# A fused decoder layer on one core: the sixteen rounds of the cross attention in another order

## The chip, the core and the metric

The kernel runs on one core of a Trainium2 chip. The core has TensorE (PE in the profile; its weight loads are PEld), VectorE (DVE), ScalarE (ACT), GpSimd (POOL) and SyncE (SP, which only issues DMAs here). Each engine works through its own queue in order, and they meet in semaphores. The metric is the device time of one execution in microseconds, the median of several runs.

## The reference

A decoder layer on 32 blocks of 128 tokens, 512 channels, in float32:

```
x = x + self_attention(layernorm(x))            # differential attention, 32 score heads of 16
x = x + cross_attention(layernorm(x), ctx)      # 8 heads of 16, 512 positions, rotary
x = x + experts(layernorm(x))                   # 32 experts, 6 of 32 per token, and a shared expert
```

In the cross attention one block has queries, keys and values of 128 channels by 512 positions. Queries and keys are rotated (`t*cos + rot(t)*sin`), the scores are softmaxed over 512 keys, the values are weighted, and an output projection and the residual follow. The experts begin with a router: scores of 32 experts, the best 2 of 4 groups, the best 6 experts, their weights (a sigmoid, divided by the sum), and a place for each token in the list of each expert.

## The kernel before

The kernel has three parts: self attention (to about 750 us), cross attention (to about 1850 us), and the experts. The cross attention takes 32 blocks b, 16 rounds each: round n has b = n // 16 and r = n % 16. `cross_round` (line 151) lists the steps of round r, and every engine goes through this list and carries out its own piece of each step, in the order of the list. So the order in `cross_round` is the order of each engine's queue. A step that doesn't belong to an engine leaves its queue alone: two steps that change places in the list change nothing on an engine that has only one of them.

Every round has one `top` and one `score`. The rest is side work, which belongs to other blocks than the round's own (b + 1 is being prepared, b - 1 closed, b - 2 projected out, b - 3 and b - 4 routed). With T, S and so on as short names for what PE does:

- T, `top`: two matmuls of 512 columns (L765) into one of two pairs of banks; DVE takes the maxima of 1024 columns (L1409). T(n) waits until DVE has reduced T(n-2).
- S, `score`: two matmuls (L787) into banks 5 and 6; ACT takes the exponent of 1024 columns (PX, L1076). S(n) waits for the exponent of S(n-1): there is one pair of banks.
- A: weights times values (L804), behind every second S; `last` is the fourth A of a half block. ACT then copies bank 7 (`copy_v`, L1136).
- K, `keys_of`: six matmuls (L620 to L622 on CXS and WV); ACT writes vh (L1127).
- `rotate`: three matmuls, then a product on DVE (T1, L1434); GpSimd adds the two products (`total`, L1797); ACT rounds (`high`, L1119); GpSimd takes the rest (`low`, L1804). SP sends the parts to memory (`away`) and back in another layout (`stack`, 6 DMAs each for a quarter).
- `shares`, `sums`, `turn_g`: four transposes (L607). `expand` is ACT's copy rc (L1143) ahead of `shares`; DVE multiplies (on, L1445). `join` is the output projection, six matmuls. `maxima`: four transposes (L774), ACT copies (NT, L1070), SP writes a row.
- `norm_m`, `high_m`, `low_m`: the normalised x of a block (ACT, L1101), rounded (ACT, XMH, L1087), and the rest (GpSimd, xmL, L1814). `high_c`, `low_c` do the same for the context (ACT L1083, GpSimd CXS L1809), and `high_o`, `low_o` for the output (ACT OS L1095, GpSimd OS L1819).
- Router: `gate` (PE L862), `narrow` and `choose` (DVE, L1462 to L1485; the last three instructions of `choose` are L1479, L1483 and L1485), `weights` (DVE, from L1490), `rank`, `places`, and `spread` 0 to 5 (one indirect DMA of GpSimd each, L1829). `stats_g` and `stats_m`: bn_stats on DVE, three small instructions on GpSimd (ve, pow, sX or sY), `norm_g` or `norm_m` on ACT.

Bank 0 is shared by all side steps of PE: each waits until the reader of the step before it is done.

```
def bank0(signal, count):
    if zero["free"]:
        pe.wait_ge(*zero["free"])
    zero["free"] = (S[signal], count)
```

The two instructions of DVE and GpSimd that the prediction speaks of most are

```
dve.tensor_tensor(RM[:, 1 - d, :], RM[:, d, :], M[:, :], ALU.add)                      # L1485, end of choose
pool.tensor_tensor(xmL[:, :], xm[:, :], XMH[:, :].bitcast(f32), ALU.subtract)          # L1814, low_m
```

and GpSimd's `low_c` waits for ACT's `high_c` of the same block (`pool.wait_ge(S["a_ch"], b + 1)`).

Of the kernel before, what the change touches and what calls it, by code (L numbers as in the profile page):

```python
# [7 lines left out]
NB = 32  # L8
# [53 lines left out]
def self_part(do, do_cross):  # L62
# [3 lines left out]
    for w in range(-9, 2 * NB + 4):  # L66
# [26 lines left out]
        if e >= 4 * NB + 8 - AHEAD:  # L93
            for n in range(2):
                cross_round(do_cross, 2 * (e - (4 * NB + 8)) + n)
# [35 lines left out]
        if o >= 4 * NB + 8 - AHEAD:  # L131
            for n in range(2):
                cross_round(do_cross, 2 * (o - (4 * NB + 8)) + n)


def cross_part(do):


    for n in range(16 * NB + 14):
        cross_round(do, n)  # L140
# [10 lines left out]
def cross_round(do, n):  # L151
    b, r = divmod(n, 16)
    if r == 0:
        if 0 <= n - LAG < 16 * NB:
            do("score", n - LAG)
        do("stats_g", b + -3)
        do("stack", b + 0, 1, 1)
        do("keys_of", b + 0, 0)
        if 0 <= n < 16 * NB:
            do("top", n)  # L160
        do("expand", b + -2, 1)
    if r == 1:
        if 0 <= n < 16 * NB:
            do("top", n)
        if 0 <= n - LAG < 16 * NB:
            do("score", n - LAG)
        do("total", b + 1, 0)
        do("maxima", b + -1, 1)
        do("narrow", b + -4)
    if r == 2:  # L170
        if 0 <= n - LAG < 16 * NB:
            do("score", n - LAG)
        if 0 <= n < 16 * NB:
            do("top", n)
        do("rotate", b + 1, 0, 0)
        do("choose", b + -4)
    if r == 3:
        if 0 <= n - LAG < 16 * NB:
            do("score", n - LAG)
        do("rotate", b + 1, 0, 1)  # L180
        do("norm_g", b + -3)
        if 0 <= n < 16 * NB:
            do("top", n)
    if r == 4:
        if 0 <= n - LAG < 16 * NB:
            do("score", n - LAG)
        do("high", b + 1, 0)
        do("load_y", b + 2)
        do("last", b + -1, 0)
        do("shares", b + -2, 1)  # L190
        if 0 <= n < 16 * NB:
            do("top", n)
    if r == 5:
        if 0 <= n - LAG < 16 * NB:
            do("score", n - LAG)
        do("low", b + 1, 0)
        do("rotate", b + 1, 1, 0)
        do("copy_v", b + -1, 0)
        if 0 <= n < 16 * NB:
            do("top", n)  # L200
    if r == 6:
        if 0 <= n - LAG < 16 * NB:
            do("score", n - LAG)
        do("load_c", b + 2)
        do("rotate", b + 1, 1, 1)
        do("high_o", b + -2, 1)
        if 0 <= n < 16 * NB:
            do("top", n)
    if r == 7:
        if 0 <= n - LAG < 16 * NB:  # L210
            do("score", n - LAG)
        do("soften", b + -4)
        do("low_o", b + -2, 1)
        do("total", b + 1, 1)
        do("sums", b + -1, 0)
        do("weights", b + -4)
        if 0 <= n < 16 * NB:
            do("top", n)
    if r == 8:
        if 0 <= n - LAG < 16 * NB:  # L220
            do("score", n - LAG)
        do("low", b + 1, 1)
        do("rank", b + -4)
        if 0 <= n < 16 * NB:
            do("top", n)
        do("expand", b + -1, 0)
    if r == 9:
        if 0 <= n - LAG < 16 * NB:
            do("score", n - LAG)
        do("high", b + 1, 1)  # L230
        do("away", b + 1, 0)
        do("maxima", b + 0, 0)
        if 0 <= n < 16 * NB:
            do("top", n)
        do("stats_m", b + 2)
    if r == 10:
        if 0 <= n - LAG < 16 * NB:
            do("score", n - LAG)
        do("shares", b + -1, 0)
        do("places", b + -4)  # L240
        if 0 <= n < 16 * NB:
            do("top", n)
    if r == 11:
        if 0 <= n - LAG < 16 * NB:
            do("score", n - LAG)
        do("spread", b + -4, 0)
        do("low_o", b + -1, 0)
        do("high_o", b + -1, 0)
        do("turn_g", b + -3)
        do("spread", b + -4, 1)  # L250
        if 0 <= n < 16 * NB:
            do("top", n)
        do("spread", b + -4, 2)
    if r == 12:
        if 0 <= n - LAG < 16 * NB:
            do("score", n - LAG)
        do("away", b + 1, 1)
        do("stack", b + 1, 0, 0)
        do("stack", b + 1, 1, 0)
        do("norm_m", b + 2)  # L260
        do("gate", b + -3)
        if 0 <= n < 16 * NB:
            do("top", n)
    if r == 13:
        if 0 <= n - LAG < 16 * NB:
            do("score", n - LAG)
        do("keys_of", b + 0, 1)
        do("stack", b + 1, 0, 1)
        do("copy_v", b + -1, 1)
        do("last", b + -1, 1)  # L270
        do("spread", b + -4, 3)
        if 0 <= n < 16 * NB:
            do("top", n)
        do("spread", b + -4, 4)
    if r == 14:
        if 0 <= n - LAG < 16 * NB:
            do("score", n - LAG)
        if 0 <= n < 16 * NB:
            do("top", n)
        do("join", b + -2)  # L280
        do("low_c", b + 2)
        do("low_m", b + 2)
        do("high_c", b + 2)
    if r == 15:
        if 0 <= n < 16 * NB:
            do("top", n)
        if 0 <= n - LAG < 16 * NB:
            do("score", n - LAG)
        do("sums", b + -1, 1)
        do("high_m", b + 2)  # L290
        do("spread", b + -4, 5)
    piece, at = divmod(n - (16 * NB - 80), 8)
    if at == 0 and 0 <= piece < 8:
        do("land", piece // 4, piece % 4)
    if n == 16 * NB - 8:
        do("rows", 0)
    if 16 * NB <= n < 16 * NB + 12:
        do("split", 0, 1)
    if 16 * NB + 12 <= n < 16 * NB + 14:
        do("split", 1, 6)  # L300
# [1903 lines left out]
```

## Time and profile before

| | us |
|---|---|
| median of 3 runs | 3828.13 (3823.77 to 3829.65) |
| the profiled execution | 3817.57 |
| its span | 3815.8 |
| one block in the middle of the cross attention | 32.95 |
| in it busy: PE / DVE / ACT / GpSimd | 32.01 / 29.16 / 25.46 / 18.30 |

A timeline row gives the start from the span's start, the duration, engine, line, operation, and in brackets the idle time before it and what ended that. Rows that follow each other closely and are alike are merged (x2, x4, x8); one float32 matmul of A or `gate` stands as two. An instruction starts up to 0.1 us before the one in front of it has ended, so intervals are taken from start to start.

### The profile page before, as it was taken

To read this page: it belongs to the slowest core of one execution; us is meant where nothing else is said; L and a number is where in the kernel's file an instruction comes from. 1 tells how busy PE (TensorE), PEld (TensorE's weight loads), DVE (VectorE), ACT (ScalarE), POOL (GpSimd) and SP (SyncE) were. 2 spreads that over 40 slices of the span, in tenths; PEclk is the share of its full clock that TensorE was granted. 3 is DMA by queue.
4 is the path that set the end of the run, shared out by engine and by line. 5 is a ranking of instruction groups with operands and counts; after the bars stand their busy time and mean duration, and the time that the engine had idled before them with its cause. 6 is when DMAs were issued, how large, how long until landed. Compare 5 with 4: busy or idle time off the path is not lost.

```text
span 3815.8 us, 74126 instructions
## 1 busy us (share of the span) xinstructions
PE 3668.1 (96%) x24778; PEld 2905.2 (76%) x24778; DVE 2883.4 (76%) x5969; ACT 2352.5 (62%) x5418; POOL 1812.3 (47%) x2121
## 2 busy tenths in 40 slices
PE   6999999789999999999899999999999999999999
PEld 6888888534444444444589999999999999999998
DVE  5888888578888888888457777777777777777333
ACT  5888888457777777777435555555555555555121
POOL 2333332334555555554326666665666665555210
PEclk9999999789999999999899999999999999999999
DMA  5000000133334444443149999999999999998421
GB/s 209 24 25 28 27 26 21 42 108 123 127 124 133 133 128 127 131 154 121 48 141 265 263 268 263 266 268 266 264 267 264 268 265 265 267 262 239 154 84 58
DMA packets 290168, 621.37 MB, mean 163 GB/s; under 512 B 70000, under 2 KB 78576, under 8 KB 289664
## 3 DMA queue, kind: packets, MB, share of 16 engines
q1 hardware_dynamic: 224640, 464.01, 37.1%
q0 software_dynamic: 64000, 150.52, 16.4%
q8 instruction: 203, 3.33, 0.4%
q10 hardware_dynamic: 1152, 2.10, 0.2%
q14 instruction: 173, 1.42, 0.1%
HBM read 459.93 MB, written 155.98 MB: 161 GB/s over the span
## 4 chain that ended last, share of the span: by engine, by line
PE 82%; ACT 7%; DVE 6%; issue 3%; SPq 2%; DMA 1%; POOL 0%; DVEq 0%; ACTq 0%; POOLq 0%
PE ps L620 18%; PE ps L622 17%; PE ps L621 17%; PE ps L804 7%; PE ps L607 4%; PE ps L765 4%; ACT PA L1009 4%; PE ps L787 4%; PE ps L725 2%; PE ps L898 2%; PE ps L924 2%; PE ps L647 2%; ACT PX L1076 1%; DVE NM L1409 1%; DVE WD L1557 1%
## 5 line engine op out<-in xcount | busy, mean ns | idle before, releaser
L620 PE MATMUL ps<-WG,XT 128*128 128x352 f32 x2304 | 765.9, 332 | 7.3 <-DVE XT L1586 4.8
L621 PE MATMUL ps<-WG,XT 128*128 128x352 f32 x2304 | 744.7, 323 | 0.0
L622 PE MATMUL ps<-WG,XT 128*128 128x352 f32 x2304 | 744.6, 323 | 0.0
L1409 DVE TENSOR_REDUCE NM<-ps 128x2 f32<-128x1024 f32 x512 | 614.2, 1217 | 98.9 <-PE ps L765 92.4
L1076 ACT ACTIVATE PX<-ps 128x1024 f32<-128x1024 f32 x512 | 523.4, 1022 | 198.7 <-PE ps L787 184.2
L1903 POOL DMA_INDIRECT sum<-YO,TI x224 | 401.3, 1792 | 488.6 <-issue 393.8
L1222 ACT ACTIVATE HS<-ps 128x352 f32<-128x352 f32 x288 | 133.6, 464 | 561.7 <-PE ps L622 561.7
L1592 DVE TENSOR_TENSOR HS<-ps,HS 128x352 f32<-128x352 f32 x288 | 150.9, 524 | 426.1 <-ACT HS L1222 422.7
L1550 DVE TENSOR_TENSOR WG<-WL,WG 128x704 fp32r<-128x704 f32 x528 | 449.7, 882 | 28.3 <-ACT WG L1189 28.2
L620 PEld LDWEIGHTS ps<-WG,XT 128*128 128x128 f32 x2304 | 434.5, 189 | 9.3 <-DVE XT L1586 6.5
L621 PEld LDWEIGHTS ps<-WG,XT 128*128 128x128 f32 x2304 | 435.0, 189 | 0.0
L622 PEld LDWEIGHTS ps<-WG,XT 128*128 128x128 f32 x2304 | 434.3, 189 | 0.0
L1189 ACT ACTIVATE WG<-WL 128x704 fp32r<-128x704 f32 x528 | 395.2, 789 | 14.1 <-DMA DL<-in_w_down 13.9
L1009 ACT ACTIVATE PA<-ps,nb 128x128 f32<-128x128 f32 x1024 | 358.0, 381 | 1.2 <-DVE nb L1278 1.2
L620 PE MATMUL ps<-WD,HT 128*128 128x512 f32 (+1 forms) x864 | 344.9, 399 | 12.3 <-DVE HT L1598 12.3
L622 PE MATMUL ps<-WD,HT 128*128 128x512 f32 (+1 forms) x864 | 341.6, 395 | 0.0
L621 PE MATMUL ps<-WD,HT 128*128 128x512 f32 (+1 forms) x864 | 341.0, 395 | 0.0
L1885 POOL DMA_INDIRECT XI<-x_normed,TI x224 | 278.7, 1244 | 80.7 <-POOL TI L1880 61.8
L1213 ACT ACTIVATE XT<-ps 128x512 fp32r<-128x512 f32 x224 | 133.3, 595 | 245.2 <-PE ps L898 238.9
L804 PE MATMUL ps<-PX,vh 128*32 128x512 f32 x2048 | 278.8, 617 | 0.0
L1557 DVE TENSOR_TENSOR WD<-DL,WD 128x1024 fp32r<-128x1024 f32 (+1 forms) x264 | 240.0, 950 | 47.9 <-ACT WD L1196 47.8
L765 PE MATMUL ps<-KS,QS 48*128 48x512 f32 x1024 | 243.6, 484 | 14.3 <-DMA QS<-kq_parts 9.1
(275 smaller groups left out, 8530.8 us busy)
## 6 DMA issues: line engine op xcount, KB each, us to landing
WL<-in_w_gate SPq DMA_DIRECT2D x128, 704.0 KB, 4.2
WL<-in_w_up SPq DMA_DIRECT2D x128, 704.0 KB, 6.0
DL<-in_w_down SPq DMA_DIRECT2D x128, 512.0 KB, 8.4
kq_parts<-HL SPq DMA_DIRECT2D x64, 512.0 KB, 3.0
KS<-kq_parts SPq DMA_DIRECT2D x384, 64.0 KB, 2.3
QS<-kq_parts SPq DMA_DIRECT2D x384, 64.0 KB, 2.4
DL<-in_w_down SPq DMA_DIRECT2D x128, 192.0 KB, 9.2
CB<-sum POOLq DMA_DIRECT2D x64, 256.0 KB, 3.0
```

Of the source, the lines that this page charges most:

```text
L620: pe.matmul(out_, lh(0), rh(0), start=first, stop=False)
L621: pe.matmul(out_, lh(0), rh(1), start=False, stop=False)
L622: return pe.matmul(out_, lh(1), rh(0), start=False, stop=last)
L765: e = pe.matmul(bank(1 + 2 * (n % 2) + i), QS[64 * i:64 * i + 48, d, pp, 128 * qc:128 * qc + 128], KS[64 * i:64 * i + 48, d, pp, :], start ...
L804: e = pe.matmul(ps[32 * j:32 * j + 32, 7 * 512:8 * 512], vh[:, b % 2, sc, 4 * hh + j, :], PX[:, (8 * g + 2 * sc + j // 2) % 4, j % 2, :], ...
L1009: e = act.activation(PA[:, d, h, :], sums[:, h, :], ACT.Exp, bias=nb4[:, d, h:h + 1], scale=0.25, accum_out=SU[:, 8 * u + h:8 * u + h + 1])
L1076: act.activation(PX[:, n % 4, :, :], ps[:, 5 * 512:7 * 512], ACT.Exp, scale=0.25).then_inc(S["a_px"], 1)
L1189: act.activation(WG[q][:, 0, w, c:c + 2, :], WL[:, q, w, c:c + 2, :], ACT.Copy).then_inc(S["a_sp"], 1)
L1409: dve.tensor_reduce(NM[:, g % 2, qc, p:4:2], ps[:, 512 * bk:512 * bk + 1024].rearrange("p (i k) -> p i k", k=512), AX.X, ALU.max, negate=T ...
L1550: dve.tensor_tensor(WG[q][:, 1, w, c:c + 2, :], WL[:, q, w, c:c + 2, :], WG[q][:, 0, w, c:c + 2, :].bitcast(f32), ALU.subtract).then_inc(S ...
L1885: pool.indirect_dma_start(out=XI[:, t % NX, :], out_offset=None, in_=XN[:, :], in_offset=bass.IndirectOffsetOnAxis(ap=TI[:, r % 8:r % 8 + ...
L1903: pool.indirect_dma_start(out=AC[r % 2][:, :], out_offset=bass.IndirectOffsetOnAxis(ap=TI[:, r % 8:r % 8 + 1], axis=0), in_=YO[:, o % NO, ...
```

## The change

Only `cross_round` changes; no instruction is added or taken out. `keys_of` of half 0 moves from round 0 to round 1, behind `top` of round 0. In round 11 `top` goes ahead of `score`. `last` of half 1 moves from round 13 to the head of round 12. In round 4 `shares` goes ahead of `last`. `high_m` and `low_m` move from rounds 14 and 15 to round 1 of the next block, `low_c` from 14 to 12, ahead of `low_o`. `spread` 2 to 5 move behind these two. `weights` goes behind `top` of round 7, and `total` moves from rounds 1 and 7 to 3 and 8. `stack` of the last quarter of the queries moves from round 0 to 4, with `norm_g` behind it, `load_y` and `load_c` from 4 and 6 to 6 and 7.

```
@@ cross_round: r == 0, r == 1 @@
         do("stats_g", b + -3)
-        do("stack", b + 0, 1, 1)
-        do("keys_of", b + 0, 0)
         if 0 <= n < 16 * NB:
             do("top", n)
         do("expand", b + -2, 1)
     if r == 1:
+        do("keys_of", b + 0, 0)
         if 0 <= n < 16 * NB:
             do("top", n)
+        do("narrow", b + -4)
+        do("high_m", b + 1)
+        do("low_m", b + 1)
         if 0 <= n - LAG < 16 * NB:
             do("score", n - LAG)
-        do("total", b + 1, 0)
         do("maxima", b + -1, 1)
-        do("narrow", b + -4)
...
@@ r == 4 @@
-        do("high", b + 1, 0)
-        do("load_y", b + 2)
+        do("stack", b + 0, 1, 1)
+        do("shares", b + -2, 1)
         do("last", b + -1, 0)
-        do("shares", b + -2, 1)
+        do("norm_g", b + -3)
         if 0 <= n < 16 * NB:
             do("top", n)
+        do("high", b + 1, 0)
...
@@ r == 7 @@
-        do("total", b + 1, 1)
         do("sums", b + -1, 0)
-        do("weights", b + -4)
         if 0 <= n < 16 * NB:
             do("top", n)
+        do("weights", b + -4)
...
@@ r == 11, r == 12 @@
+        if 0 <= n < 16 * NB:
+            do("top", n)
+        do("spread", b + -4, 0)
         if 0 <= n - LAG < 16 * NB:
             do("score", n - LAG)
-        do("spread", b + -4, 0)
-        do("low_o", b + -1, 0)
-        do("high_o", b + -1, 0)
         do("turn_g", b + -3)
         do("spread", b + -4, 1)
-        if 0 <= n < 16 * NB:
-            do("top", n)
-        do("spread", b + -4, 2)
     if r == 12:
+        do("low_c", b + 2)
+        do("away", b + 1, 1)
+        do("stack", b + 1, 0, 0)
+        do("high_o", b + -1, 0)
+        do("stack", b + 1, 1, 0)
+        do("low_o", b + -1, 0)
+        do("last", b + -1, 1)
         if 0 <= n - LAG < 16 * NB:
             do("score", n - LAG)
...
@@ r == 13 to 15 @@
+        do("spread", b + -4, 2)
         do("spread", b + -4, 3)
-        do("spread", b + -4, 4)
+        do("norm_m", b + 2)
...
-        do("low_c", b + 2)
-        do("low_m", b + 2)
+        do("spread", b + -4, 4)
```

What this makes of PE's queue in rounds 10 to 13 (from `shares` to `keys_of`; the rows `x4` of L765 are two T in a row):

```order
 L607 MATMUL ps<-CST,rc 128x128 x4
-L765 MATMUL ps<-KS,QS 128x512 x2
+L765 MATMUL ps<-KS,QS 128x512 x4
 L787 MATMUL ps<-QS,KS 128x512 x2
 L804 MATMUL ps<-PX,vh 32x512 x4
 L607 MATMUL ps<-CST,x 128x128 x4
-L765 MATMUL ps<-KS,QS 128x512 x2
+L804 MATMUL ps<-PX,vh 32x512 x4
 L787 MATMUL ps<-QS,KS 128x512 x2
 L862 MATMUL ps<-GW,x3T 128x32 x4
```

T of round 11 went ahead of S, and `last` (the second L804) stands in T's old place, between `turn_g` and S of round 12. In round 4 PE's queue reads:

```order
 L765 MATMUL ps<-KS,QS 128x512 x2
 L787 MATMUL ps<-QS,KS 128x512 x2
-L804 MATMUL ps<-PX,vh 32x512 x4
 L607 MATMUL ps<-CST,rc 128x128 x4
+L804 MATMUL ps<-PX,vh 32x512 x4
 L765 MATMUL ps<-KS,QS 128x512 x2
 L787 MATMUL ps<-QS,KS 128x512 x2
```

The transposes of `shares` now come right behind S, and `last` behind them. GpSimd's queue before, from `stats_m` (ve, sX) of one block to `total` of the next:

```order
404 L1760 TENSOR_SCALAR sX<-mv,sX 128x1
405 L1829 DMA xs_beside<-e,SI 131072x80
406 L1819 TENSOR_TENSOR OS<-on,OS 128x512
407 L1829 DMA xs_beside<-e,SI 131072x80 x4
408 L1809 TENSOR_TENSOR CXS<-cx,CXS 128x512
409 L1814 TENSOR_TENSOR xmL<-xm,XMH 128x512
410 L1829 DMA xs_beside<-e,SI 131072x80
411 L1753 TENSOR_SCALAR ve<-mv 128x1
412 L1755 TENSOR_TENSOR sY<-ve,mh 128x1
413 L1760 TENSOR_SCALAR sY<-mv,sY 128x1
414 L1797 TENSOR_TENSOR T<-T 128x512
```

and of the changed kernel:

```order
400 L1760 TENSOR_SCALAR sX<-mv,sX 128x1
401 L1829 DMA xs_beside<-e,SI 131072x80 x2
402 L1809 TENSOR_TENSOR CXS<-cx,CXS 128x512
403 L1819 TENSOR_TENSOR OS<-on,OS 128x512
404 L1829 DMA xs_beside<-e,SI 131072x80 x4
405 L1753 TENSOR_SCALAR ve<-mv 128x1
406 L1755 TENSOR_TENSOR sY<-ve,mh 128x1
407 L1760 TENSOR_SCALAR sY<-mv,sY 128x1
408 L1814 TENSOR_TENSOR xmL<-xm,XMH 128x512
409 L1797 TENSOR_TENSOR T<-T 128x512
```

`low_c` (L1809) now has four of the six spreads behind it, and `low_m` (L1814) comes behind all of them and behind `stats_g`, directly ahead of `total`.

## Rows read from the trace of the kernel before

**Rows 1.** One block: length, busy time by engine (instructions), clock, DMA share.

```profile
1399.90:1432.85 32.95, 32.01 (x202) 15.15 (x202) 29.16 (x55) 25.46 (x35) 18.30 (x21) 1.00 0.41 128
```

**Rows 2.** Timeline of PE in this block: start, duration, idle before.

```profile
1407.03 0.49 PE L787 MATMUL ps<-QS,KS 49*128 49x512 f32 x2
...
1409.48 0.39 PE L787 MATMUL ps<-QS,KS 49*128 49x512 f32 x2
1409.99 1.05 PE L862 MATMUL ps<-GW,x3T 128*128 128x32 f32 x8
...
1411.30 0.40 PE L787 MATMUL ps<-QS,KS 49*128 49x512 f32 x2
...
1412.54 1.06 PE L804 MATMUL ps<-PX,vh 128*32 128x512 f32 x8
...
1418.29 0.50 PE L787 MATMUL ps<-QS,KS 49*128 49x512 f32 x2
...
1427.76 0.65 PE L607 MATMUL ps<-CST,rc 128*128 128x128 f32 x4
...
1429.29 0.47 PE L620 MATMUL ps<-XMH,WXH 128*128 128x512 f32 x1 [0.21 <-DVE on L1445]
...
1434.28 0.50 PE L765 MATMUL ps<-KS,QS 48*128 48x512 f32 x2
```

**Rows 3.** Timeline of DVE, rounds 8, 9 and 2.

```profile
1404.41 2.52 DVE L1409 TENSOR_REDUCE NM<-ps 128x2 f32<-128x1024 f32 x2
...
1424.34 0.74 DVE L1434 SCALAR_TENSOR_TENSOR T<-ps,BX,CST 128x512 f32<-128x512 f32 x1
...
1425.95 0.19 DVE L1485 TENSOR_TENSOR RM<-RM,M 128x32 f32<-128x32 f32 x1
1426.20 0.75 DVE L1434 SCALAR_TENSOR_TENSOR T<-ps,BX,CST 128x512 f32<-128x512 f32 x1
```

**Rows 4.** Timeline of ACT, rounds 8, 12 and 13.

```profile
1403.04 0.62 ACT L1143 ACTIVATE rc<-R 128x512 f32<-128x512 f32 x1
...
1410.83 0.81 ACT L1101 ACTIVATE xm<-XB,sX 128x512 f32<-128x512 f32 x1
1411.74 1.02 ACT L1076 ACTIVATE PX<-ps 128x1024 f32<-128x1024 f32 x1
1412.66 0.38 ACT L1127 ACTIVATE vh<-ps 128x256 f32<-128x256 f32 x1
1413.67 0.60 ACT L1136 ACTIVATE ox<-ps 128x512 f32<-128x512 f32 x1 [0.63 <-PE ps L804]
```

**Rows 5.** Timeline of GpSimd (POOL) in this block.

```profile
1410.44 1.30 POOL L1819 TENSOR_TENSOR OS<-on,OS 128x512 fp32r<-128x512 f32 x1
1411.90 0.99 POOL L1829 DMA_INDIRECT xs_beside<-e,SI  x1 [0.17 <-issue]
...
1415.73 0.96 POOL L1829 DMA_INDIRECT xs_beside<-e,SI  x1 [0.30 <-issue]
...
1419.88 0.98 POOL L1829 DMA_INDIRECT xs_beside<-e,SI  x1
1420.94 0.23 POOL L1753 TENSOR_SCALAR ve<-mv 128x1 f32<-128x1 f32 x1
...
1421.93 0.27 POOL L1760 TENSOR_SCALAR sY<-mv,sY 128x1 f32<-128x1 f32 x1
```

**Rows 6.** L1490: durations from 1000 to 1780, then its group from 1860 to 1960.

```profile
L1490 DVE TENSOR_SCALAR SG<-SG x24: 546/546/564, 1006.4 to 1764.7; 128x32 f32<-128x32 f32 x24
...
L1490 DVE TENSOR_SCALAR SG<-SG 128x32 f32<-128x32 f32 x3 | 0.5, 181 | 3.6 <-ACT SG L1155 3.6
```

**Rows 7.** Timeline of the self attention, GpSimd and DVE.

```profile
300.50 1.15 DVE L1312 SCALAR_TENSOR_TENSOR aw<-PA,CC 128x128 f32<-128x128 f32 x4
...
307.07 2.18 DVE L1312 SCALAR_TENSOR_TENSOR aw<-PA,CC 128x128 f32<-128x128 f32 x4
...
307.80 1.30 POOL L1782 TENSOR_TENSOR oTL<-oT,OTH 128x512 fp32r<-128x512 f32 x1 [6.01 <-ACT OTH L985]
```

More of the change, by code:

```diff
@@ L180, in cross_round @@
         do("rotate", b + 1, 0, 1)
-        do("norm_g", b + -3)
+        do("total", b + 1, 0)
         if 0 <= n < 16 * NB:
@@ L195, in cross_round @@
             do("score", n - LAG)
+        do("copy_v", b + -1, 0)
+        do("rotate", b + 1, 1, 0)
         do("low", b + 1, 0)
-        do("rotate", b + 1, 1, 0)
-        do("copy_v", b + -1, 0)
         if 0 <= n < 16 * NB:
@@ L203, in cross_round @@
             do("score", n - LAG)
-        do("load_c", b + 2)
         do("rotate", b + 1, 1, 1)
-        do("high_o", b + -2, 1)
         if 0 <= n < 16 * NB:
             do("top", n)
+        do("high_o", b + -2, 1)
+        do("load_y", b + 2)
     if r == 7:
@@ L211, in cross_round @@
             do("score", n - LAG)
+        do("low_o", b + -2, 1)
         do("soften", b + -4)
-        do("low_o", b + -2, 1)
-        do("total", b + 1, 1)
+        do("load_c", b + 2)
         do("sums", b + -1, 0)
-        do("weights", b + -4)
         if 0 <= n < 16 * NB:
             do("top", n)
+        do("weights", b + -4)
     if r == 8:
+        do("total", b + 1, 1)
+        do("low", b + 1, 1)
         if 0 <= n - LAG < 16 * NB:
             do("score", n - LAG)
-        do("low", b + 1, 1)
         do("rank", b + -4)
+        do("expand", b + -1, 0)
         if 0 <= n < 16 * NB:
             do("top", n)
-        do("expand", b + -1, 0)
     if r == 9:
@@ L239, in cross_round @@
         do("shares", b + -1, 0)
-        do("places", b + -4)
         if 0 <= n < 16 * NB:
             do("top", n)
+        do("places", b + -4)
     if r == 11:
+        if 0 <= n < 16 * NB:
+            do("top", n)
+        do("spread", b + -4, 0)
         if 0 <= n - LAG < 16 * NB:
             do("score", n - LAG)
-        do("spread", b + -4, 0)
-        do("low_o", b + -1, 0)
-        do("high_o", b + -1, 0)
         do("turn_g", b + -3)
         do("spread", b + -4, 1)
-        if 0 <= n < 16 * NB:
-            do("top", n)
-        do("spread", b + -4, 2)
     if r == 12:
+        do("low_c", b + 2)
[5 more added lines that the diff above has]
+        do("last", b + -1, 1)
         if 0 <= n - LAG < 16 * NB:
             do("score", n - LAG)
[L257 to L260, printed above, removed]
         do("gate", b + -3)
@@ L267, in cross_round @@
         do("keys_of", b + 0, 1)
+        if 0 <= n < 16 * NB:
+            do("top", n)
         do("stack", b + 1, 0, 1)
         do("copy_v", b + -1, 1)
-        do("last", b + -1, 1)
+        do("spread", b + -4, 2)
         do("spread", b + -4, 3)
-        if 0 <= n < 16 * NB:
-            do("top", n)
-        do("spread", b + -4, 4)
+        do("norm_m", b + 2)
     if r == 14:
@@ L279, in cross_round @@
             do("top", n)
+        do("high_c", b + 2)
         do("join", b + -2)
-        do("low_c", b + 2)
-        do("low_m", b + 2)
-        do("high_c", b + 2)
+        do("spread", b + -4, 4)
     if r == 15:
@@ L289, in cross_round @@
         do("sums", b + -1, 1)
-        do("high_m", b + 2)
         do("spread", b + -4, 5)
```

## The prediction

> **What bounds the kernel now.** I read the busy time by engine first, then one block of the cross attention engine by engine. In a block of 32.95 us PE is busy 32.01, DVE 29.16, ACT 25.46 and GpSimd 18.30 [rows 1]. So PE nearly bounds this part, and there is no engine to relieve: an order can only take away PE's short waits, or add some. In PE's timeline [rows 2] they are seen as intervals longer than usual between two starts, such as S of round 12 to `gate`, 1409.48 to 1409.99: 0.51 us where 0.33 would do, because ACT had not yet copied x3T. By adding up such excesses over the block (0.1 to 0.35 each) I get about 2 us, 2 x 28 = 56 us over the 28 full blocks (4 to 31). That is the most that any order can bring. The self attention and the experts, three quarters of the time, keep their order.
>
> I walk one block of the new order with the old durations. Below, times from 1400 on are of the trace, and those with a plus count from the start of a named instruction.
>
> **Rounds 10 to 15: a gain.** T of round 11 now stands ahead of S. It must wait until DVE has reduced T of round 9. That pair of reductions ends at 1404.41 + 2.52 = 1406.93 [rows 3]; moving `weights` behind T's reduction of round 7 does not change this end, since the second of the pair then waits for its matmuls. So T goes at 1407.0 and S, a third of a microsecond later, at 1407.34 instead of 1407.03 [rows 2]. From S of round 11 to S of round 13 it took 4.27 (to 1411.30). Now T is not in it (0.34 less), `gate` finds x3T ready (0.18 less), S is no longer the first after a wait (0.13 less), and `last` is in it, 1.06 long and 1.00 from start to start [rows 2]: 4.62, so S of round 13 at 1411.96. From there to S of round 0 it was 6.99 (to 1418.29) with `last` inside; now 5.99, at 1417.95. Gain 0.34 a block.
>
> **Rounds 0 to 6: most of it stays, as long as nothing else happens.** Counted from S of round 0 (+0): `keys_of` moves behind T, the sum of PE's work is the same. On ACT the exponent is now followed by rc, vh and XMH before the next exponent can start: +0.54, then 0.92, 0.52, 0.28 and 0.52 (durations of 1.02, 0.62, 0.38, 0.62 [rows 4], each 0.10 less from start to start), so +2.78; S of round 2 at +3.86 instead of +3.76. The `rotate` behind it waits for ACT's NT in either order and stays at +4.61 (before 4.60), and the product of the second `rotate` starts on DVE at +7.93, as before (1426.20 - 1418.29 = 7.91 [rows 3]). In round 4 `shares` now stands directly behind S and needs bank 0, that is the end of this product: 7.93 + 0.75 [rows 3] + 0.14 for the signal (my estimate; the rows show 0.1 to 0.2 in such places) = +8.82, where PE was ready at +8.49. PE waits 0.33 there; `last`, which covered it before, comes after. In exchange `last` covers what the third `rotate` waited for, DVE's product `on` (0.28 [rows 2]). From `shares` to T of round 7 it took 6.52 (1427.76 to 1434.28); now 6.52 + 1.00 - 0.28 = 7.24, so T at +16.06 against +15.99: loss 0.07. Net gain 0.27 a block, 0.27 x 28 = 7.6 us.
>
> `weights` itself: L1490 takes 546 ns in all 24 blocks and 181 ns in the tail, where GpSimd is idle beside it [rows 6]. The 0.37 us comes back, and buys nothing: PE doesn't wait for DVE between rounds 7 and 10 now. If it did, it would be 0.37 x 28 = 10 us; I take zero.
>
> **What hides the rest.** SP's queue: `stack` of the last quarter now waits behind `maxima` and is issued some 4 us later, but T of round 8 needs it about 10 us after that. T of round 0 comes 1.7 us earlier in the block than before, and its `stack` is issued from SP's queue at the old time; I put its cost between 0 and 0.5 us a block and take 0. `norm_g` and `high` sit between two exponents in round 4: 0.3 us to spare.
>
> **GpSimd's new order: the loss.** `low_c` now waits in GpSimd's queue for `high_c` of round 14, and `low_o` and four spreads wait behind it, `stats_g` behind these, and then `low_m`. Counted from S of round 13: exponent +0.44 (1411.30 to 1411.74 [rows 2, 4]), then vh, ox and norm_m in a row (intervals of 0.92, 0.28, 0.50, 0.71 by the durations of [rows 4]) and the exponent of round 14 at +2.85; `high_c` behind it ends at +4.39, `low_c` starts at +4.47, `low_o` 1.23 later at +5.70. From a `low_o` to the next spread 1.46, three more 1.28 apart ((1415.73 - 1411.90) / 3), from the last to ve 1.06, to the end of sY 1.26 [rows 5]: 5.70 + 1.46 + 3.83 + 1.06 + 1.26 = +13.31. So `low_m` starts at +13.3 and lasts 1.28.
>
> DVE, from the same S: S of round 0 at +5.99, S of round 2 at 5.99 + 3.86 = +9.85, T 0.34 later, its reduction 0.44 after that (as the exponent after S), the first product 1.13 later (half of the pair of 2.52, less the 0.1 of overlap [rows 3]), L1485 (the last instruction of `choose`) 1.61 after this one's start [rows 3]: +13.37. It would end 0.2 later, and the second product needs DVE only at 5.99 + 7.93 = +13.92.
>
> So L1485 starts within a tenth of the start of `low_m`, on the wrong side by this sum. What happens then is in the trace: four aw on DVE (two operands in SBUF, as L1485) take 1.15 us, but 2.18 where GpSimd's oTL starts at 307.80 under them [rows 7]; they end at 309.25, just behind GpSimd's 309.10. L1490 shows the same with one operand [rows 6]. The later of the two is held to the other's end. L1485 would end near 13.31 + 1.28 + 0.07 = +14.66, and the second product starts 0.74 later than +13.92. `shares` waits on it, with nothing in front to cover it: 0.74 on PE. Net 0.74 - 0.27 = 0.47 a block.
>
> The Trainium skill (SBUF — State Buffer, "SBUF: two separate sides") says that VectorE with two SBUF inputs and GpSimd take a shared pair of ports for the whole instruction, and that whichever starts first has it. By that rule, the trace agrees (aw). The Trainium skill's page GPSIMD Engine Reference ("Key points") only speaks of contention on these interfaces; read as a shared rate, a doubled L1485 would end 0.2 later, inside the 0.35 that DVE has to spare, and the time would be the rival's below. The row decides for the whole instruction.
>
> **The sum,** against the profiled execution of 3817.57 (span 3815.8): 28 x 0.47 = +13.2; blocks 0 to 3 have no `choose`, 4 x 0.27 = -1.1; the tail, where `last` now fills PE's wait ahead of `gate`, -1.5; the seam into the cross attention, by estimates of mine, where `keys_of` leaves a gap of PE, +0.8, and wo no longer waits for GpSimd's `total`, -0.8. Together +10.6, 3828.2 in that execution. It ran 10.56 below the median of 3828.13, so 3838.7 as a median, 3839.
>
> **The rivals.**
> - *No collision (the other side, faster).* `low_m` starts 0.1 us later than my sum, or L1485 earlier, and GpSimd starts behind it. Then 28 x -0.27 - 1.1 - 1.5 = -10: 3818. It decides at 0.06 us; any delay in GpSimd's four spreads speaks for it, any delay of PE or ACT in rounds 13 to 2 against it, for L1485 then only moves further into `low_m`, whose 1.28 us it can't pass. With L1485 late by a whole us the hold would shrink again.
> - *Gains cancel.* No collision, but the new waits (T of round 11 on DVE, `shares` on the product, S of round 2 on ACT) are each 0.1 longer than summed, or T of round 0 waits 0.2 to 0.3 for `stack`: 0 a block, 3826.
> - *The change doesn't do what it says:* `weights` stays under a GpSimd instruction. GpSimd's `total` in front of it starts as before and DVE comes 1.4 us later, so I hold this for unlikely; alone it would change nothing.
> - *Worse:* collision and T of round 0 late by 0.3: +8 more, 3847.
>
> **How the numbers follow.** Collision 0.45, with 3839; no collision and faster 0.33, 3818; cancelling 0.15, 3826; worse 0.07. About 0.2% (7.7 us) is what a measurement tells from no change. Faster by more than that needs nearly the whole of the 0.27 a block, and part of the 0.33 falls short of it; a collision in some blocks only gives any value between. Faster 0.32, same 0.22, slower 0.46. The forecast's own range is 3833 to 3846; with the rival of the other side 3814 to 3846.
>
> **What would show it.** L1485 at about 1.2 to 1.4 us instead of 0.19 in 28 blocks, L1490 at 0.18; GpSimd's L1814 beside L1485; PE's L607 of rc with an idle time of about 1 us "<-DVE T L1434"; a block of 33.4. If L1485 stays at 0.19 the block should be 32.7, and my forecast is wrong in the order of two starts. If L787 of round 11 doesn't come ahead by the 0.34 summed up at round 0, the first part is wrong.

## The result, and the profile after

The changed kernel takes 3832.09 us (median of 20 runs, 3827.86 to 3840.00), the kernel before on the same chip 3823.26 (20 runs, 3818.83 to 3832.23): ratio 1.0021, 95% interval [1.0015, 1.0027]. It is slower by 0.2%, 8.8 us. The forecast was 3839, in a range of 3833 to 3846, or 3814 to 3846 with the rival of the other side; 3832.09 lies 0.9 below the first of the two. As a change, +10.6 was forecast and +8.8 measured.

The profiled execution took 3830.47 (span 3828.7), 12.9 more than the one of before. One block of the changed kernel, from T of round 7 to the next (columns as in [rows 1]):

```profile
1441.50:1475.01 33.51, 32.15 (x200) 15.16 (x200) 29.21 (x53) 25.23 (x34) 18.13 (x21) 1.00 0.40 126
```

The busy times are those of before; the block is 0.6 longer than its 32.93. PE's timeline shows where, with the rows that answer to [rows 2]: T ahead of S in round 11, `last` (the second L804), S of round 12, `gate`, S of round 13, S of round 0, the wait ahead of `shares`, T of round 7.

```profile
1446.67 0.92 PE L765 MATMUL ps<-KS,QS 48*128 48x512 f32 x4
1447.43 0.40 PE L787 MATMUL ps<-QS,KS 49*128 49x512 f32 x2
1447.76 1.06 PE L804 MATMUL ps<-PX,vh 128*32 128x512 f32 x8
...
1449.43 1.06 PE L804 MATMUL ps<-PX,vh 128*32 128x512 f32 x8
1450.43 0.50 PE L787 MATMUL ps<-QS,KS 49*128 49x512 f32 x2
1450.86 1.08 PE L862 MATMUL ps<-GW,x3T 128*128 128x32 f32 x8
...
1452.21 0.40 PE L787 MATMUL ps<-QS,KS 49*128 49x512 f32 x2
...
1458.23 0.50 PE L787 MATMUL ps<-QS,KS 49*128 49x512 f32 x2
...
1467.76 0.63 PE L607 MATMUL ps<-CST,rc 128*128 128x128 f32 x4 [0.56 <-DVE T L1434]
...
1475.01 0.50 PE L765 MATMUL ps<-KS,QS 48*128 48x512 f32 x2
```

DVE in round 2 of this block, the rows that answer to the last three of [rows 3]:

```profile
1463.56 1.23 DVE L1409 TENSOR_REDUCE NM<-ps 128x2 f32<-128x1024 f32 x1 [1.18 <-PE ps L765]
1464.70 0.74 DVE L1434 SCALAR_TENSOR_TENSOR T<-ps,BX,CST 128x512 f32<-128x512 f32 x1
1465.36 0.18 DVE L1474 TENSOR_TENSOR LM<-LM,KP 128x32 f32<-128x32 f32 x1
1465.57 0.20 DVE L1477 MAX8 m<-LM 128x8 f32<-128x34 f32 x1
...
1465.88 0.18 DVE L1479 MATCH_REPLACE8 LM<-m,LM 128x34 f32<-128x34 f32 x1
1466.10 0.63 DVE L1483 TENSOR_SCALAR M<-LM 128x32 f32<-128x32 f32 x1
1466.76 0.19 DVE L1485 TENSOR_TENSOR RM<-RM,M 128x32 f32<-128x32 f32 x1
1466.87 0.74 DVE L1434 SCALAR_TENSOR_TENSOR T<-ps,BX,CST 128x512 f32<-128x512 f32 x1
```

GpSimd beside it (answers to [rows 5]): the spreads of rounds 13 to 15 in a row, and `low_m` behind them.

```profile
1456.65 1.28 POOL L1809 TENSOR_TENSOR CXS<-cx,CXS 128x512 fp32r<-128x512 f32 x1 [3.91 <-ACT CXS L1083]
...
1461.87 0.96 POOL L1829 DMA_INDIRECT xs_beside<-e,SI  x1 [0.30 <-issue]
1463.13 0.96 POOL L1829 DMA_INDIRECT xs_beside<-e,SI  x1 [0.31 <-issue]
...
1465.38 1.31 POOL L1814 TENSOR_TENSOR xmL<-xm,XMH 128x512 fp32r<-128x512 f32 x1
```

There is the collision. `low_m` runs from 1465.38 to 1466.69, L1483 of `choose` is held to 1466.73, and the second product starts at 1466.87, 14.66 behind S of round 13. PE waits for it ahead of `shares`. (The idle time in its row is 0.56, not the "about 1 us" of the forecast: PE came there 0.4 later than summed, for it had waited for the late first product. In the block from 1175.5, where that product is not late, it is 0.75.) The holds over all blocks, by duration (minimum, median, maximum in ns):

```profile
L1483 DVE TENSOR_SCALAR M<-LM x23: 182/630/1292, 1028.6 to 1768.4; 128x32 f32<-128x32 f32 x23
L1490 DVE TENSOR_SCALAR SG<-SG x24: 170/172/173, 1005.6 to 1779.6; 128x32 f32<-128x32 f32 x24
```

L1490 is free (0.55 before, [rows 6]), L1485 too (192 ns in all blocks). In three blocks of the trace (1242.6, 1377.5 and 1613.6, by their NT) the hold falls on L1474, at the head of `choose`:

```profile
1633.61 1.32 DVE L1474 TENSOR_TENSOR LM<-LM,KP 128x32 f32<-128x32 f32 x1
```

`low_m` had started there at 1633.60, 0.01 ahead. All of `choose` (0.9 us) then still follows the hold, and the block is 34.26 to 34.29 long instead of 33.5. (Two expectations below speak of four such blocks. In the fourth, 34.05 long, L1483 is held, and `low_m` itself starts 0.5 later than usual.)

One thing in these rows was not in the forecast: the reduction at 1463.56 starts 0.75 us after its matmuls have ended (1462.81), and DVE was idle. This happens in 19 of the blocks; I call it a late start. In most of them it cost nothing, for the end of `low_m` decides in any case: the blocks whose reduction is not late (those from 1175.5, 1344.0, 1647.9 and the next three) are 33.49 to 33.53 long as well, with L1483 held for 1.26 to 1.29. But the three blocks with L1474 held owe their 0.7 to it: L1474 starts 20.0 us after NT there, together with `low_m`, and at 19.3 where nothing is late. Late starts cost a good deal elsewhere, as the experiments show.

### The profile page after: what moved, and what is told of

It reads as the page before. It is cut to its first block, busy times and chain, and to the rows that moved or that the text cites. A ratio compares the mean times of both kernels' runs of the same rounds, so it can differ in the third digit from the quotient of the medians.

```text
span 3828.7 us, 74126 instructions
## 1 busy us (share of the span) xinstructions
PE 3667.2 (96%) x24778; PEld 2903.3 (76%) x24778; DVE 2891.6 (76%) x5969; ACT 2348.7 (61%) x5418; POOL 1802.3 (47%) x2121
## 4 chain that ended last, share of the span: by engine, by line
PE 70%; ACT 9%; POOL 7%; issue 7%; DVE 5%; SPq 1%; DMA 1%; DVEq 0%; ACTq 0%; POOLq 0%
PE ps L620 16%; PE ps L622 16%; PE ps L621 16%; ACT PA L1009 4%; PE ps L804 4%; PE ps L607 3%; PE ps L725 2%; PE ps L898 2%; PE ps L765 2%; PE ps L787 2%; PE ps L924 2%; ACT PX L1076 2%; POOL xs_beside L1829 2%; PE ps L647 2%; DVE WD L1557 1%
## 5 line engine op out<-in xcount | busy, mean ns | idle before, releaser
L1903 POOL DMA_INDIRECT sum<-YO,TI x224 | 398.6, 1780 | 495.1 <-issue 398.6
L804 PE MATMUL ps<-PX,vh 128*32 128x512 f32 x2048 | 277.7, 615 | 0.3
L765 PE MATMUL ps<-KS,QS 48*128 48x512 f32 x1024 | 246.5, 484 | 14.5 <-DMA QS<-kq_parts 11.2
```

Source lines behind the costliest of these rows:

```text
L765: e = pe.matmul(bank(1 + 2 * (n % 2) + i), QS[64 * i:64 * i + 48, d, pp, 128 * qc:128 * qc + 128], KS[64 * i:64 * i + 48, d, pp, :], start ...
L804: e = pe.matmul(ps[32 * j:32 * j + 32, 7 * 512:8 * 512], vh[:, b % 2, sc, 4 * hh + j, :], PX[:, (8 * g + 2 * sc + j // 2) % 4, j % 2, :], ...
L1903: pool.indirect_dma_start(out=AC[r % 2][:, :], out_offset=bass.IndirectOffsetOnAxis(ap=TI[:, r % 8:r % 8 + 1], axis=0), in_=YO[:, o % NO, ...
```

## The experiments

In all of them times are compared with the kernel before in runs on the same chip; three chips were used, and the kernel before took 3837.16, 3826.48 and 3824.80 on them. A block is the median distance of every second NT in ACT's timeline.

**1. The hold taken away.** The last two spreads of a block go behind `low_m` in GpSimd's queue (the last block's stay).

```
 r == 1:   do("low_m", b + 1)
+          do("spread", b + -5, 4); do("spread", b + -5, 5)
 r == 14:  -  do("spread", b + -4, 4)
 r == 15:  -  do("spread", b + -4, 5)
```

> The changed kernel with one thing different: the last two `spread` of a block stand behind `low_m` in GpSimd's queue (round 1 of the next block) and not ahead of it. In the changed kernel `low_m` (L1814) runs 20.00 to 21.30 us after NT and every hold on DVE (L1483, in four blocks L1474) ends with it. Two spreads of 1.27 us less in front of it put it at about 17.5 to 18.8, where `choose` has its wait for T's matmuls and its PSUM operations; the first operation of `choose` with both operands in SBUF starts at 19.3 at the earliest. Theory (the hold alone makes the changed kernel slow): no hold, the second product at 20.8 instead of 21.5, PE waits 0.33 instead of 1.07 ahead of rc, block 32.8 instead of 33.55, and 0.7 more in the four blocks with L1474 held: 28 x 0.74 + 4 x 0.72 = 23.6 less than the changed kernel, about 3809. If the 0.75 us by which the reduction of round 2 starts late stays, the product is only 0.35 earlier: 3820. Rival (the exposed `shares` and the new waits of rounds 11 to 13 make it slow, the hold is covered): block 33.5, 3832 as the changed kernel.

Measured: 3818.05, ratio 0.9948 [0.9934, 0.9961]; block 32.87; no hold on `choose` in any block, and no late start in round 2. `choose` on DVE in one block:

```profile
1421.68 0.18 DVE L1474 TENSOR_TENSOR LM<-LM,KP 128x32 f32<-128x32 f32 x1
...
1422.64 0.19 DVE L1485 TENSOR_TENSOR RM<-RM,M 128x32 f32<-128x32 f32 x1
1423.21 0.75 DVE L1434 SCALAR_TENSOR_TENSOR T<-ps,BX,CST 128x512 f32<-128x512 f32 x1 [0.39 <-issue]
```

with `low_m` done before it:

```profile
1419.89 1.28 POOL L1814 TENSOR_TENSOR xmL<-xm,XMH 128x512 fp32r<-128x512 f32 x1
```

These rows are of its second set of runs, beside the changed kernel on one chip:

> The changed kernel itself, unaltered, so that it stands beside the others on one chip. In the last set the kernel before took 3837 where it had taken 3823, and its two near copies had blocks of 33.4 and 34.0 in place of 32.93, each with an exponent or a reduction that started 0.6 to 1.0 us after its matmuls had ended, just behind the third or fourth `spread` in a row. If that is a matter of the chip, the changed kernel against the kernel before may stand at 1.002 again or, where the kernel before has these late starts, at 0.999 to 1.000. Its own block should be 33.5 in either case, since its late starts (round 2) are hidden by the hold, whose end `low_m` sets.

> The changed kernel with the last two `spread` behind `low_m`, as run before (block 32.87, no hold, no late start). Theory (the hold costs 0.68 a block, and no kernel with two `spread` in a row at most has late starts): 3818, 0.995 to 0.996 of the changed kernel on the same chip. Rival (its 0.9948 was the chip's and not the order's): within 0.1% of the changed kernel.

Measured: the changed kernel 3835.38, ratio 1.0029 [1.0018, 1.0039]; the one without the hold 3807.86, ratio 0.9956 [0.9943, 0.9970]. The difference of 27.5 us is a little above the 23.6 summed: the block goes from 33.54 to 32.82 (0.72, times the 26 blocks with a hold is 19), and the longer blocks of the changed kernel, those with L1474 held among them (six in this profile, one of them 35.78 long, 5.8 together above the others), go too. That the hold makes the changed kernel slow is shown. The edit also breaks up the row of spreads and with it the late starts of rounds 2 and 3, but these can't be the cause of the 0.7: five held blocks of the changed kernel have neither, and they are as long as those with them. The rival, that the waits in rounds 4 and 11 to 13 make it slow, has fallen: they are all still in.

**2. `last` ahead of `shares` again, with the hold.**

```
 r == 4:  -  do("shares", b + -2, 1)
             do("last", b + -1, 0)
          +  do("shares", b + -2, 1)
```

> The changed kernel with `last` again ahead of `shares` in round 4 on PE. Collision and GpSimd's order stay. Theory (the end of `low_m` is a fixed time, and what it costs is what PE has nothing to cover with): S of round 4 at 8.57 us after S of round 0, `last` behind it to 9.9, `shares` at 9.9 without a wait, the third `rotate` waits 0.3 again: 6.52 from there to T of round 7, so 16.4 instead of 16.8, 0.37 less a block; in the four blocks with the longer hold 0.4 more: 10 to 12 less than the changed kernel, 3821. Rival (the wait only moves to the third `rotate`, whose product is as late as before): 3832.

Measured: 3839.23, ratio 1.0004 [0.9995, 1.0013]. The changed kernel was not run on this chip, where the kernel before took 3837 instead of 3823, so the times alone don't decide; the trace does. In blocks with the same hold as in the changed kernel (L1483) the gain is there: 32.97, 33.20 and 33.24 instead of 33.5, 0.3 to 0.5 where 0.37 was summed. But there are only these three of 26; in 20 L1474 is held, the product starts at 22.2 us after NT instead of 21.5, and most of these blocks are 33.7 long. (In the other three, of 34.8, the reduction itself starts 2.4 late; why is open.) Which instruction of `choose` meets `low_m` hangs on 0.01 to 0.5 us, and a change elsewhere turns it. The sum was about right for a fixed hold, and the hold was not fixed.

**3. The order without the hold, `last` ahead of `shares`.** The edits of 1 and 2 together.

> The changed kernel without the hold (two `spread` behind `low_m`), and with `last` again ahead of `shares` in round 4. There PE waits 0.34 ahead of `shares` for the end of the second product and 0.22 ahead of the fourth `rotate`. Theory (`last` hides the 0.34, and the third `rotate` then waits for `on` by about as much, 0.28 as before): block 32.75 to 32.95, within 0.1% of the kernel with the move alone (32.82). Rival (DVE has no time to spare in rounds 3 to 6, and `on` comes 0.66 later): 0.3 to 0.4 a block slower.

Measured: 3805.95, ratio 0.9953 [0.9941, 0.9965]; block 32.77 (32.82 with `shares` first). A tie, as expected: `shares` ahead of `last` costs nothing by itself. With a hold it does: a block with L1483 held is 33.2 long with `last` in front (experiment 2) and 33.5 without it, so this move makes about 0.3 of the 0.7, and the hold costs about 0.4 even behind the cover.

**4. Half of step 1:** only the last spread goes behind `low_m`.

> The changed kernel with only the last `spread` behind `low_m`, half of the step that removed the hold. `low_m` then runs from 18.7 to 20.0 us after NT. Theory (the later starter is held to the other's end, and the hold costs what it goes past the time at which the second product could start, 20.8): L1474 of `choose`, due at 19.3, is held to 20.05; the 1.3 us of `choose` behind it end at 21.1, the second product 0.3 later than 20.8: block 33.15, 3826. If the reduction of round 2 is late by 0.75 as in the changed kernel, L1474 starts at 20.0, 0.05 before the end: hardly held, but all of `choose` 0.7 later, the product at 21.2 to 21.5: 33.3 to 33.5. Rival (any overlap costs the whole of a GpSimd instruction, 1.3): 33.9.

Measured: 3820.85, ratio 0.9987 [0.9978, 0.9996]. Its blocks are of two kinds, both foreseen and both a little shorter than expected: 33.0 in six where L1474 is held for about 0.76 us,

```profile
1196.07 0.76 DVE L1474 TENSOR_TENSOR LM<-LM,KP 128x32 f32<-128x32 f32 x1
```

beside `low_m`, which started ahead of it:

```profile
1195.50 1.28 POOL L1814 TENSOR_TENSOR xmL<-xm,XMH 128x512 fp32r<-128x512 f32 x1
```

and 33.25 in the 20 blocks with the late start, where nothing is held. So `low_m` placed 0, 1.27 and 2.54 us earlier gives blocks of 33.5, 33.0 to 33.25, and 32.8. In the first kind the product starts 20.95 us after NT instead of 20.8, and the block is 0.2 longer: the cost is what the hold, with the rest of `choose` behind it, leaves past the time at which PE could have the product, and not the overlap of 0.76.

**5. Single parts put into the kernel before.** `total` of the first half from round 1 to round 3:

> The kernel before with `total` of the first half moved from round 1 to behind the second `rotate` in round 3; in the steady blocks GpSimd has nothing between the two places, so only the first rounds, beside the end of the self attention, can change. Theory (the 6.3 us that the changed kernel has ahead at the first T come from this: the product with wo no longer waits for GpSimd's oTL behind `total`, and PE's clock doesn't fall there): first NT at 777.4 instead of 782.7, blocks at 32.93, 3817.5. Rival (they come from other steps that the change moves in rounds 0 to 6, `keys_of` and `stack` among them): first NT at 782.7, 3823. My forecast had put a gain of 0.8 on this wait.

and `weights` behind `top` in round 7:

> The kernel before with `weights` behind `top` in round 7 and nothing else. L1490 should take 0.18 us instead of 0.55 in all blocks. Theory (DVE has slack between rounds 7 and 10): block 32.93, time as before, 3823, within 0.1%. Rival (those 0.37 us were on the path, as the move was meant to use): 28 x 0.37 = 10 less, 3813. Third: T's reduction first brings T of round 9 forward, gain of 0.1 to 0.2 a block, 3820.

Measured: 3838.04, ratio 0.9999 [0.9990, 1.0008], and 3834.78, ratio 0.9998 [0.9989, 1.0007]. `weights` alone is worth nothing, with L1490 at 170 ns in all blocks: DVE had the time. `total` gave a first NT at 779.5, between both expectations, and no time. The 5.4 us that the changed kernel's profile has ahead at the seam (first NT 777.4 against 782.7) are for the most part no property of the order: the same kernel (of experiment 1) had it at 783.7 and at 779.4 on two chips, the kernel before at 782.7 and 779.2, the changed kernel at 777.4 and 780.1. What differs is the granted clock between 730 and 740 us: at 0.50 to 0.52 (the kernel before, experiment 1) the first NT comes at 782.7 and 783.7, at 1.00 (the changed kernel, the kernel before again, experiment 1 again, `total` alone) at 777.4 to 779.5, and at 0.65 (the changed kernel again) at 780.1. In PE's timeline of the changed kernel the product with wo runs at 2.4 GHz,

```profile
733.28 0.39 PE L620 MATMUL ps<-WH,OTH 128*128 128x512 f32 x1
```

and in that of the kernel before at 1.2 GHz, twelve such matmuls long:

```profile
736.99 0.80 PE L620 MATMUL ps<-WH,OTH 128*128 128x512 f32 x1 [0.87 <-POOL oTL L1782]
737.59 0.63 PE L621 MATMUL ps<-WBL,OTH 128*128 128x512 f32 x1
```

Both had PE wait for 0.9 us several times ahead of it; the wait for `total` (0.87, in the row) is the one that the change takes away. What made the clock differ in otherwise equal orders stays open.

The kernels of `total` and `weights` alone showed something else: blocks of 33.4 and 34.0, where the profile of the kernel before has 32.93 throughout. That led to the next two.

**6. The kernel before, two of its four spreads in a row moved** (the fourth and fifth of a block to round 2 of the next):

```
 r == 13:  -  do("spread", b + -4, 3)
           -  do("spread", b + -4, 4)
 r == 2:      do("rotate", b + 1, 0, 0)
           +  do("spread", b + -5, 3); do("spread", b + -5, 4)
```

> The kernel before with the last two of its four `spread` in a row moved to round 2 of the next block, where GpSimd is idle for 4.8 us. Nothing else. Theory (the late starts come with three or four of them in a row, and only there): no start later than 0.3 us, block 32.93, 3818 to 3824 whatever the kernel before takes beside it; on a chip on which that takes 3837, 0.996. Rival (the late starts are a matter of the place in the block, or of DMA traffic from SP's queue at that time, and not of GpSimd's): exponents of round 15 late as before, 1.000. A third (they go with the two that now stand beside `choose`): new late starts in round 3.

Measured: 3813.07, ratio 0.9969 [0.9956, 0.9981]; blocks of 32.93, two late starts in the whole trace. And the kernel before itself, profiled again:

> The kernel before, unaltered, for a profile of it on the chip on which the others run. The one at hand (3817.57, 6 to 19 below the medians of three sets) has not one late start. Moving two of its four `spread` took 0.31% off it in the last set, though in that profile they cost nothing. Theory (the four in a row cost the kernel before some 10 us in most executions, and the profile at hand was a lucky one): this profile has exponents of round 15 that start 0.6 to 1 us late in many of the 28 blocks, blocks of 33.4 to 34.0. Rival (the gain of that move has another source): blocks of 32.93, no late start.

Measured: 3823.97, ratio 1.0002 [0.9993, 1.0012]; the median block is 33.35, and 24 exponents of round 15 are late. In one of them, PE's S of round 15 has ended at 1452.29:

```profile
1451.89 0.40 PE L787 MATMUL ps<-QS,KS 49*128 49x512 f32 x2
...
1454.22 0.50 PE L787 MATMUL ps<-QS,KS 49*128 49x512 f32 x2 [0.35 <-ACT PX L1076]
```

and ACT, idle for 1.76 us, starts its exponent 0.85 later:

```profile
1453.14 1.02 ACT L1076 ACTIVATE PX<-ps 128x1024 f32<-128x1024 f32 x1 [1.76 <-PE ps L787]
```

just after GpSimd's fourth spread in a row:

```profile
1449.96 0.96 POOL L1829 DMA_INDIRECT xs_beside<-e,SI  x1 [0.30 <-issue]
1451.22 0.96 POOL L1829 DMA_INDIRECT xs_beside<-e,SI  x1 [0.31 <-issue]
1452.21 1.29 POOL L1809 TENSOR_TENSOR CXS<-cx,CXS 128x512 fp32r<-128x512 f32 x1
```

So the profile from which I predicted (3817.57, no late start) was better than this one; that most executions have late starts is argued from the gain of experiment 6, not shown, since only two were profiled. Late starts cost the kernel before 0.42 in the median block and 8.9 us over the 27 blocks from the fourth on; the changed kernel has them too, for the most part under the hold.

**7. All four spreads in one row elsewhere,** in the kernel before:

```
 r == 11:  -  do("spread", b + -4, 1); do("spread", b + -4, 2)
 r == 13:  -  do("spread", b + -4, 3); do("spread", b + -4, 4)
 r == 2:      do("rotate", b + 1, 0, 0)
           +  do("spread", b + -5, k)  for k = 1 to 4
```

> The kernel before with all four `spread` (the second to the fifth) moved in one row to round 2, where GpSimd is idle from 22 to 27 us. Theory (a start that is released about the end of the third or fourth `spread` in a row is 0.6 to 1.0 us late, wherever they stand): no late exponent in round 15, but late ones of round 3 or 4 in most blocks, block 33.2 to 33.9, 3820 to 3838. Rival (only the place in round 15 matters, by SP's transfers of `stack` there): block 32.93, 3813 as with two moved. `total` of round 3 may come 0.1 later by the longer row, which costs nothing.

Measured: 3934.54, ratio 1.0287 [1.0274, 1.0300]; block 37.55. A miss, and by my own oversight: `total` of the first half stands in round 1, ahead of them in GpSimd's queue, and waits for a product of round 3. The four ran behind it, 25.3 to 30.2 us after NT and not from 17 on (the expectation's 22 to 27 are 1422 to 1427 in the trace of before), and pushed `low`, `low_o` and the second `total` together. These three came to lie over `weights`, back to back:

```profile
1504.42 1.28 POOL L1804 TENSOR_TENSOR HL<-T,HL 128x512 fp32r<-128x512 f32 x1
1505.65 1.27 POOL L1819 TENSOR_TENSOR OS<-on,OS 128x512 fp32r<-128x512 f32 x1
1506.88 1.26 POOL L1797 TENSOR_TENSOR T<-T 128x512 f32<-128x512 f32 x1
```

DVE's L1490, the one that took 0.55 in the kernel before, started 0.09 before the end of the first and was held through the other two:

```profile
1505.61 2.59 DVE L1490 TENSOR_SCALAR SG<-SG 128x32 f32<-128x32 f32 x1
```

PE waited 1.98, and its matmuls behind the wait ran at 1.2 GHz for a while (1.01 for the transposes that take 0.60; the granted clock of the ten us from 1510 is 0.66, the column before the DMA share):

```profile
1510.66 1.01 PE L774 MATMUL ps<-CST,NM 128*4 128x128 f32 x4 [1.98 <-DVE SV L1506]
```

```profile
1510.00:1520.00 10.00, 9.22 (x44) 4.58 (x44) 7.40 (x15) 5.24 (x7) 4.03 (x6) 0.66 0.41 121
```

A whole block of this kernel (columns as in [rows 1]):

```profile
1474.17:1511.72 37.55, 34.73 (x200) 16.08 (x200) 31.37 (x53) 25.47 (x35) 18.25 (x20) 0.91 0.35 113
```

PE is busy 34.73 for the work that took it 32.01 [rows 1], and idle 2.8 instead of 0.9. So of the 4.6 that the block has grown by, 2.7 are busy time (the slower clock) and 1.9 idle time (the longer wait). The kernel had no late start, but it can't tell of them: what would have been released beside the row no longer stood there.

**8. The part of rounds 11 to 13 alone,** on the kernel of experiment 6:

```
 r == 11:  + do("top", n)
              do("score", n - LAG)
           -  do("high_o", b + -1, 0)
           -  do("top", n)
 r == 12:  +  do("high_o", b + -1, 0)
           +  do("last", b + -1, 1)
              do("score", n - LAG)
           -  do("norm_m", b + 2)
 r == 13:  -  do("last", b + -1, 1)
           +  do("norm_m", b + 2)
```

> The kernel before with two `spread` moved to round 2 (3813, block 32.93) and in addition the part of the change in rounds 11 to 13 alone: T ahead of S in round 11, `last` ahead of S in round 12, `high_o` behind turn_g, `norm_m` in round 13. Rounds 0 to 6 and the rest of GpSimd's order as before. My forecast gave this part 0.34 a block: block 32.59, 28 x 0.34 = 9.5 less, 3803. The changed kernel's own stretch from T of round 10 to S of round 0 came out 0.16 shorter (11.56 against 11.72): block 32.77, 4.5 less, 3808. Rival (the gain is given back by GpSimd's later `low_o` or by T of round 13): 3813.

Measured: 3806.68, ratio 0.9946 [0.9933, 0.9958]; block 32.75, so 0.18 less than 32.93, not 0.34. No hold and no late start. With experiments 1 and 3 it is a version that beats both kernels, the kernel before by 0.5%; the three can't be told apart.

## Why the prediction came out as it did

The likeliest case was the right one: GpSimd's `low_m` under `choose`, DVE held to its end, `shares` without cover. Step by step:

- *From T of round 10 to S of round 0.* S of round 11 is 0.76 behind T of round 10, as summed (0.77). From it to S of round 13 the sum was 4.62, measured 4.78: this term was mis-sized. S of round 12 is now the first behind `last`, and `gate` follows it by 0.43 and not 0.33, so that it gives back 0.08 and not 0.18; the other 0.06 are hundredths of several intervals. The gain of this part is 0.16 and not 0.34 (0.18 in experiment 8).
- *S of round 13 to S of round 0:* 5.99 summed, 6.02 measured.
- *S of round 0 to `shares`:* 8.82 + 0.74 = 9.56 summed, 9.53 measured. The second product was to start 14.66 behind S of round 13; it did so to 0.01. Within this, two things were off and did not matter: DVE was 0.73 later than summed (the late start), and so L1483 was held, not L1485. The end of `low_m` is what counts, and that was summed to 0.1.
- *`shares` to T of round 7:* 7.24 summed, 7.25 measured. Without the hold (experiment 1) PE waits the 0.34 ahead of `shares` that the forecast had (0.33).
- *The block:* 33.40 forecast, 33.51 to 33.55 measured. What is over comes from rounds 11 to 13. The three blocks with L1474 held (0.7 each) were not foreseen; the text spoke of a start decided by 0.06 us, but for L1485 alone.
- *`weights`:* 0.37 back and nothing gained, as said; shown by experiment 5.
- *Blocks 0 to 3, seam, tail:* forecast -1.1, 0 and -1.5. The first three blocks took 1.4 more; the second takes 32.1 instead of 31.4 in experiment 8 too, so it belongs to rounds 11 to 13, where T's new place has no `gate` behind it to fill the wait (the last is argued, not shown). The first NT came 5.4 earlier, mostly by the clock. From the 31st block on, -0.7.
- *The sum:* +10.6 forecast, +12.9 measured in the profiled executions, made of 17.6 (27 blocks), 1.4, -5.4 and -0.7. The hold's place was right. That the total came out so near is in part luck: with the seam at 0, as forecast, it would be +18.3.
- *From the profiled execution to the median.* This step failed. I added the 10.56 by which the profile of before lay under its median, and so came to 3839; the changed kernel's profile lies only 1.6 under its own. Of the 8.9 between the two, 4.9 come from the median itself: 3828.13 was that of three runs, and over 20 runs it is 3823.26. With that one the same sum gives 3833.9. The other 4.1 are that the profile of before still lay 5.7 under the better median. Late starts are a likely part of it: the second profile of before, 5.9 longer than the first, has 8.9 more in the 27 blocks and 3.5 less at the seam. The changed kernel loses little by them, since its hold covers them except in the blocks with L1474 held. Against that second profile, with blocks of 33.35, the change costs 0.2 a block and not 0.6.

The rival of no collision was 3818, that is 0.9973 of the kernel before; experiment 1 is 0.9948 and 0.9956. It gives more, because it also has no four spreads in a row.

## What to carry to other kernels

When an instruction of one engine can be held by another's, compute the end of the holder and the moment at which the held engine's result is next needed: the cost is the distance, whatever is held in between. Look at what stands in front of the waiting step on the bottleneck engine, since an edit that takes that cover away makes the same hold cost more (0.7 a block instead of 0.4 here). And before converting a sum into a median, ask of how many runs the median is, and whether the profiled execution shows all the delays that the others have; in a queue, read also what stands ahead of the place to which something is moved.

## What the runs showed of the hardware

- *Late starts.* An idle ACT or DVE often starts 0.5 to 1.0 us (1.4 and 2.4 in a few cases) after its matmuls have ended, when they end about the end of the third or fourth indirect DMA in a row on GpSimd (the changed kernel: 19 reductions of round 2 and 20 exponents of round 3; experiment 4, three in a row: 20 reductions; the kernel before, second profile: 24 exponents of round 15). With two in a row there were none or up to three in a trace, though in experiment 1 some 50 idle exponents a trace had their matmuls end within 0.25 us of the end of the second. The kernel before had none in one profile and 24 in another. What delays them stays open: no run here took the indirect DMA away, or separated it from its transfers.
- *One operand can be enough.* L1483 and L1490 (TENSOR_SCALAR), with one tensor read and written in SBUF, are held as L1474 with two. L1477 (MAX8) and L1479 (MATCH_REPLACE8), which also read one tensor in SBUF, are not: they keep their 0.20 and 0.18 wholly beside `low_m`, in 16 blocks of the changed kernel. Reductions from PSUM beside the same GpSimd instructions keep their 1.22. The Trainium skill (SBUF — State Buffer, "SBUF: two separate sides") names two kinds of VectorE operation that take the shared pair, one with two SBUF inputs and one in a 2-port perf mode. The first covers L1474, held for 1.32; the hold of L1483 and L1490 fits the second, but no view here shows in which mode an operation ran.
- *A hold spans several instructions.* With no gap between them, GpSimd's three operations in experiment 7 kept L1490 for 2.59, from the end of the first to that of the third: the waiting engine did not get in between.
- *The price of a long wait includes the clock.* PE's wait of 1.98 in experiment 7 was followed by 10 us at a granted clock of 0.66, part of it at 1.2 GHz. PE's busy time in the block rose by 2.7, more than its idle time did (1.9).
